# A four-layer attention and feed-forward network on one core: inputs by batch, and a new order around the first router

## What is computed

```python
# layer 0, attention (per batch)
x = einsum('bdn,bdm->bnm', Q, K) / sqrt(dk)      # Q: normalised x, K: ctx
score = sigmoid(x)
out = einsum('bvn,bnm->bvm', V, score)           # V: ctx; out is added to x

# layer 0, mixture of experts (16 experts, 4 chosen for each token)
logits = x @ router_weight.T + router_bias       # x: second normalisation
top_val, top_idx = top_k(logits, 4); top_val = softmax(top_val)
gate_up = einsum('th,ehd->etd', x, gate_up_proj) + gate_up_proj_bias
out = sum over e of score[t,e] * (down_proj_e((up + 1) * gate * sigmoid(1.702 * gate)) + bias)

# layer 3, attention: the keys on the context, which the kernel computes early
kvx = einsum('bsi,oi->bso', cond, w_kv_x); kx, vx = split(kvx); kx = _ln(kx.reshape(b, sc, g, d), ...)
```

## Time and profile before

| | |
|---|---|
| median of 3 runs | 1167.55 us (1164.51 to 1169.42) |
| the profiled execution's own time | 1166.6 us |
| its span | 1164.8 us |
| mean granted clock of TensorE | 0.944 |
| busy: PE, PEld, DVE, ACT, POOL | 88%, 75%, 74%, 54%, 47% of the span |
| chain that ended last, by engine | PE 64%, DVE 19%, ACT 10%, issue 4%, POOL 1%, DMA 1% |
| instructions | 18816 |

### The profile page before, as it was taken

How to read it: one execution, slowest core, us unless ns; L and a number is a source line. 1 busy time by engine, 2 the same in 40 slices (tenths; PEclk the granted TensorE clock), 3 DMA queues, 4 the chain that set the end, 5 groups by cost and what they waited for, 6 DMA issues and landing times.

```text
span 1164.8 us, 18816 instructions
## 1 busy us (share of the span) xinstructions
PE 1026.3 (88%) x6446; PEld 872.4 (75%) x6446; DVE 862.2 (74%) x2151; ACT 628.7 (54%) x1656; POOL 549.5 (47%) x413
## 2 busy tenths in 40 slices
PE   4999999999995897877488599999999999999976
PEld 4648888888884684545255488899889988999955
DVE  4436777777778544569887688888888888888873
ACT  1474444444432353577845477676666667675621
POOL 2316766577642221101233565655746575645550
PEclk9899999999997898878798799999999999999998
DMA  6003011111000101000000000001010101000101
GB/s 253 1 1 104 28 55 46 37 55 55 28 1 25 37 17 37 36 2 1 12 8 19 24 31 19 20 1 55 1 38 2 55 2 37 2 19 1 74 0 37
DMA packets 13680, 37.14 MB, mean 32 GB/s; under 512 B 1345, under 2 KB 5521, under 8 KB 12945
## 3 DMA queue, kind: packets, MB, share of 16 engines
q1 hardware_dynamic: 13584, 35.93, 9.3%
HBM read 34.88 MB, written 1.05 MB: 31 GB/s over the span
## 4 chain that ended last, share of the span: by engine, by line
PE 64%; DVE 19%; ACT 10%; issue 4%; POOL 1%; DMA 1%; SPq 0%; DVEq 0%; ACTq 0%; POOLq 0%
PE bank L680 15%; PE bank L700 7%; PE bank L2041 6%; PE bank L2064 6%; PE bank L1979 6%; ACT y L2187 3%; PE bank L1954 3%; PE bank L1990 3%; PE bank L1041 2%; DVE g_ql L1913 2%; PE bank L1056 1%; PE bank L1968 1%; PE bank L490 1%; DVE g_bs L2345 1%; PE bank L491 1%
## 5 line engine op out<-in xcount | busy, mean ns | idle before, releaser
L2187 ACT ACTIVATE y<-bank,g_mx 128x256 f32<-128x256 f32 x256 | 117.5, 486 | 98.6 <-DVE g_mx L2357 98.6
L2476 POOL TENSOR_TENSOR y<-y,g_sm 128x1024 f32<-128x1024 f32 x64 | 120.0, 1895 | 21.9 <-DVE g_sm L2365 21.9
L2453 POOL TENSOR_TENSOR g_c<-arena 128x1024 fp32r<-128x1024 f32 x30 | 64.1, 2136 | 115.7 <-DVE arena L2289 115.7
L2064 PE MATMUL bank<-arena 128*128 128x256 f32 x512 | 116.1, 379 | 0.0
L718 ACT ACTIVATE arena<-arena 128x512 f32<-128x512 f32 x64 | 40.4, 633 | 126.2 <-DVE arena L799 126.2
L2064 PEld LDWEIGHTS bank<-arena 128*128 128x128 f32 x512 | 94.9, 190 | 12.0 <-issue 0.2
L680 PE MATMUL bank<-b_yh,b_wh 128*128 128x512 f32 x256 | 102.6, 401 | 0.0
L680 PE MATMUL bank<-b_yl,b_wh 128*128 128x512 f32 x256 | 101.9, 398 | 0.0
L680 PE MATMUL bank<-b_yh,b_wl 128*128 128x512 f32 x256 | 101.6, 397 | 0.0
L2041 PE MATMUL bank<-g_qh,g_xs 128*128 128x256 f32 x256 | 68.0, 301 | 22.3 <-POOL g_xs L2420 15.8
L753 POOL TENSOR_TENSOR b_hl<-arena,b_hh 128x512 fp32r<-128x512 f32 x64 | 81.4, 1293 | 9.0 <-ACT b_hh L727 9.0
(11 more groups left out here) (380 smaller groups left out, 3139.9 us busy)
## 6 DMA issues: line engine op xcount, KB each, us to landing
arena<-in_dram SPq DMA_DIRECT2D x37, 512.0 KB, 3.6
arena<-in_dram SPq DMA_DIRECT2D x17, 256.0 KB, 3.8
arena<-in_dram SPq DMA_DIRECT2D x3, 1024.0 KB, 4.9
cx<-in_dram SPq DMA_DIRECT2D x2, 1024.0 KB, 8.2
arena<-in_dram SPq DMA_DIRECT2D x2, 704.0 KB, 7.3
x<-in_dram SPq DMA_DIRECT2D x1, 1024.0 KB, 5.6
cxT<-in_dram SPq DMA_DIRECT2D x1, 1024.0 KB, 11.2
out_dram<-x SPq DMA_DIRECT2D x4, 256.0 KB, 2.2
```

Of the source, the lines that this page charges most:

```text
L2064: m = pe.matmul(o[:, st * 256:st * 256 + 256], g_t[:, c, st * P:st * P + P], keys, start=True, stop=True)
L2187: m = act.activation(g_p[:, c, st, :], o[:, st * 256:st * 256 + 256], ACT.Exp, bias=g_mx[j % 2][:, 2 * c + st:2 * c + st + 1], accum_out=g ...
L2453: pool.tensor_tensor(cat, g_o[j % 2], g_om, ALU.subtract).then_inc(s_gc, 1)
L2476: pool.tensor_tensor(pf, pf, sums, ALU.mult).then_inc(s_gp, 1)
```

## The change

On SyncE the three inputs come in by batch (x, `cx`, `cxT` of batch 0, then of batch 1, and so on), the constants behind them, `rows` last; each has a semaphore of its own. On the DVE, `A_dve` now holds both normalisations and the additions by batch: each batch of the first normalisation is opened and scaled before the next, and the second normalisation of a batch is opened right after its addition. `setup_dve` and `G_consts_dve` stand in `B_dve` behind the routing steps, `K_centre_dve` behind the opening of batch 0 of the second normalisation. On POOL the centring of the key weights comes in two parts between batches of the second normalisation, and the all-reduce behind the first expert's low part. On TensorE the router's 16 matmuls of 16 columns become two rows of two matmuls with 512 columns and 16 output partitions, copied by ACT to `b_sT` and transposed back by eight transposes; the first six key products stand between them.

```diff
@@ setup_dve @@
-            dve.wait_ge(s_cst, 48)
+            dve.wait_ge(s_cst, 16)
...
-            dve.wait_ge(s_ctxT, 16)
+            for b in range(B):
+                dve.wait_ge(s_ctxT[b], 16)
@@ A_pe @@
-            pe.wait_ge(s_ctx, 16)
-            pe.wait_ge(s_ctxT, 16)
-            pe.wait_ge(s_cst, 48)
...
                     o = claim(pe, ("A", "s", b))
+                    pe.wait_ge(s_ctx[b], 16)
                     pe.wait_ge(s_y, 8 * K_A + 2 * b + 2)
...
                     have(pe, ("A", "s", c))
+                    pe.wait_ge(s_ctxT[c], 16)
@@ A_dve @@
+        def A_add_dve(dve, b):
+            o = take(dve, ("A", "o", b))
+            xb = x[:, 2 * b:2 * b + 2, :].rearrange("p t d -> p (t d)")
+            empty(dve.tensor_tensor(xb, xb, o[:, :], ALU.add), ("A", "o", b))
+            have(dve, ("A", "o", b))
+
         def A_dve(dve, V):
             for b in range(B):
-                o = take(dve, ("A", "o", b))
-                xb = x[:, 2 * b:2 * b + 2, :].rearrange("p t d -> p (t d)")
-                empty(dve.tensor_tensor(xb, xb, o[:, :], ALU.add), ("A", "o", b))
-            for b in range(B):
-                have(dve, ("A", "o", b))
+                dve.wait_ge(s_x[b], 16)
+                ln_open_batch(dve, V, b)
+                if b == B - 1:
+                    A_add_dve(dve, 0)
+                ln_scale(dve, K_A, b)
+            ln_open_batch(dve, V, 0)
+            K_centre_dve(dve, V)
+            ln_scale(dve, K_B, 0)
+            A_add_dve(dve, 1)
+            ln_open_batch(dve, V, 1)
+            A_add_dve(dve, 2)
+            ln_open_batch(dve, V, 2)
+            ln_scale(dve, K_B, 1)
+            A_add_dve(dve, 3)
+            ln_open_batch(dve, V, 3)
+            ln_scale(dve, K_B, 2)
+            ln_scale(dve, K_B, 3)
@@ K_centre_pool @@
-        def K_centre_pool(pool):
+        def K_centre_pool(pool, part):
             pool.wait_ge(s_kcs, 1)
-            for k in range(KD):
+            for k in (part,):
@@ B_pe @@
-            yt_pe(pe, K_B, "B")
+            def logits(h):
+                o = claim(pe, ("B", "lgT", h))
+                have(pe, ("B", "yt", 2 * h))
+                have(pe, ("B", "yt", 2 * h + 1))
+                for k in range(KD):
+                    m = pe.matmul(o[0:NE, :], b_rw[:, k, :], yT[:, k, h * 512:h * 512 + 512], start=(k == 0),
+                                  stop=(k == 1))
+                fill(m, ("B", "lgT", h))
+
+            pe.wait_ge(s_cst, 16)
             pe.wait_ge(s_small, 32)
+            yt_pe(pe, K_B, "B", range(3))
+            logits(0)
+            K_raw_pe(pe, 0)
+            K_raw_pe(pe, 1)
+            yt_pe(pe, K_B, "B", (3,))
+            K_raw_pe(pe, 2)
+            logits(1)
+            K_raw_pe(pe, 3)
             o = claim(pe, ("B", "lg"))
-            for b in range(B):
-                have(pe, ("B", "yt", b))
+            have(pe, ("B", "lgT", 0))
+            have(pe, ("B", "lgT", 1))
             for t in range(T):
-                for k in range(KD):
-                    m = pe.matmul(o[:, t * NE:t * NE + NE], yT[:, k, t * P:t * P + P], b_rw[:, k, :],
-                                  start=(k == 0), stop=(k == 1))
+                m = pe.transpose(o[:, t * NE:t * NE + NE], b_sT[0:NE, t * P:t * P + P], ident[0:NE, 0:NE])
             fill(m, ("B", "lg"))
+            for n in range(4, K_EARLY):
+                K_raw_pe(pe, n)
@@ B_act @@
-            yt_act(act, "B")
+            def logits(h):
+                o = take(act, ("B", "lgT", h))
+                empty(act.copy(b_sT[0:NE, h * 512:h * 512 + 512], o[0:NE, :]), ("B", "lgT", h))
+
+            yt_act(act, "B", range(3))
             split_y_act(act, 0)
+            logits(0)
+            K_raw_act(act, 0)
+            K_raw_act(act, 1)
+            yt_act(act, "B", (3,))
+            K_raw_act(act, 2)
             split_e_act(act, 0)
+            logits(1)
+            K_raw_act(act, 3)
             split_y_act(act, 1)
-            for n in range(K_EARLY, 11):
+            for n in range(4, 11):
                 K_raw_act(act, n)
@@ B_pool @@
             split_e_pool(pool, 0)
+            ctx_quant_pool(pool, C)
             K_rstd_pool(pool, C, 0)
@@ B_dve @@
             dve.tensor_tensor(lgf, lgf, b_m8[:, :, 0:1].to_broadcast([P, T, NE]), ALU.subtract).then_inc(s_blg, 1)
             V.sync()
+            setup_dve(dve, V)
+            G_consts_dve(dve, V)
             dve.wait_ge(s_bex, 1)
@@ block.sync @@
-            sp.dma_start(x[:, :, :], x_d.rearrange("b (h p) d -> p (b h) d", p=P)).then_inc(s_x, 16)
+            for b in range(B):
+                t2, ts_ = slice(2 * b, 2 * b + 2), slice(256 * b, 256 * b + 256)
+                sp.dma_start(x[:, t2, :], x_d[b].rearrange("(h p) d -> p h d", p=P)).then_inc(s_x[b], 16)
+                sp.dma_start(cx[:, t2, :], ctx_d[b].rearrange("(h p) d -> p h d", p=P)).then_inc(s_ctx[b], 16)
+                sp.dma_start(cxT[:, :, ts_], ctxT_d[:, :, ts_]).then_inc(s_ctxT[b], 16)
             sp.dma_start(cst[:, :], cst_d).then_inc(s_cst, 16)
-            sp.dma_start(cols[:, :], cols_d).then_inc(s_cst, 16)
-            sp.dma_start(rows[:, :], rows_d.partition_broadcast(P)).then_inc(s_cst, 16)
-            sp.dma_start(cx[:, :, :], ctx_d.rearrange("b (h p) d -> p (b h) d", p=P)).then_inc(s_ctx, 16)
-            sp.dma_start(cxT[:, :, :], ctxT_d).then_inc(s_ctxT, 16)
+            sp.dma_start(cols[:, :], cols_d).then_inc(s_cols, 16)
             sp.dma_start(k_w, wkx_d).then_inc(s_kw, 16)
             sp.dma_start(b_rw[:, :, :], rw_d).then_inc(s_small, 16)
             sp.dma_start(b_bd[0:NE, :], bd_d).then_inc(s_small, 16)
+            sp.dma_start(rows[:, :], rows_d.partition_broadcast(P)).then_inc(s_rows, 16)
@@ programs of the engines @@
-            for n in range(K_EARLY):
-                K_raw_pe(pe, n)
...
-            dve.wait_ge(s_x, 16)
-            ln_dve(dve, V, K_A)
-            setup_dve(dve, V)
-            K_centre_dve(dve, V)
-            G_consts_dve(dve, V)
             A_dve(dve, V)
             done()
-            ln_dve(dve, V, K_B)
             B_dve(dve, V)
...
             ln_pool(pool, C, K_A, EPS)
-            ctx_quant_pool(pool, C)
-            K_centre_pool(pool)
-            ln_pool(pool, C, K_B, EPS)
+            ln_pool(pool, C, K_B, EPS, batches=(0,))
+            K_centre_pool(pool, 0)
+            ln_pool(pool, C, K_B, EPS, batches=(1,))
+            K_centre_pool(pool, 1)
+            ln_pool(pool, C, K_B, EPS, batches=(2, 3))
```

More of the change, by code:

```diff
@@ L200, in build @@
         s_dve, s_act, s_pool = sem("dve_done"), sem("act_done"), sem("pool_done")
-        s_x, s_ctx, s_ctxT, s_cst = sem("x_loaded"), sem("ctx_loaded"), sem("ctxT_loaded"), sem("cst_loaded")
+        s_x, s_ctx, s_ctxT = ([sem(f"{n}_loaded{b}") for b in range(B)] for n in ("x", "ctx", "ctxT"))
+        s_cst, s_cols, s_rows = sem("cst_loaded"), sem("cols_loaded"), sem("rows_loaded")
         s_stage, s_out = sem("stage_done"), sem("stored")
@@ L468, in K_centre_dve @@
         def K_centre_dve(dve, V):
+            dve.wait_ge(s_cols, 16)
             k0 = COLS["kw"][0]
@@ L597, in build @@
             plan(("B", "yt", b), b % 4)
+        for h in range(2):
+            plan(("B", "lgT", h), 6 + h)
         plan(("B", "lg"), 6)
@@ L758, in B_dve @@
             o = take(dve, ("B", "lg"))
+            dve.wait_ge(s_rows, 16)
             lgf = b_lg[:, :, :]
@@ L2825, in _ @@
             A_act(act)
-            for n in range(K_EARLY):
-                K_raw_act(act, n)
             B_act(act)
```

## The result

| | before | after |
|---|---|---|
| median, us (runs) | 1166.92 (4, 1164.51 to 1169.42) | 1157.90 (4, 1157.58 to 1159.03) |
| the profiled execution's own time | 1166.6 | 1157.58 |
| its span | 1164.8 | 1155.8 |
| mean granted clock of TensorE | 0.944 | 0.948 |

The changed kernel takes 0.9936 of the time before (95% interval 0.992 to 0.9952), a saving of 0.64% or 7.5 us (the two medians alone would give 0.9923). The forecast of 1163.5 us, a saving of 3.1 us, had the sign right and under half of the size. The side on which it fell, faster by over 0.5%, had been given 0.32.

A forecast was written before the change was run, and what follows sets the result against it. TensorE bounds the kernel almost unbroken from 14.93 us, a transfer before. Ten products at 31.7 + 20.2 + 4.5 + 0.7 = 57.1, 3.1 us earlier: 1166.6 to 1163.5 us; own range 1161.5 to 1165.5, 8-in-10 range 1158.5 to 1167.5.

The forecast's parts named there:

- Part 1, the first y: Loads by batch: first y at 9.98 us, first attention matmul from 14.93 to 10.0, 4.9 us gained.
- rival 1: GpSimd ready early: its first configuration costs nothing, another 2.7 us saved at the start, 1160.8 us; chance 0.25.
- if the first costs the same: GpSimd's first configuration costing 6.7 us like two others: ready at 7.8 at the earliest; 8.10 taken.
- The spacing of the batches: First normalisation on the DVE: batches one after another at 3.05 us each.
- Part 2, the uncovered normalisation: Second normalisation, no longer hidden: TensorE idles some 4 us, first router row at 31.7, the 4.9 us lead gone.
- Rival 4: Second normalisation's DVE and GpSimd chain 2 to 4 us longer, router row slips as much; about 1166.5 us; chance 0.1.
- Part 3, low clock: From first router row to ten products: TensorE's clock falls after idling, adding 4.5 us to 20.2 of work.
- rival 3: Low clock before the ten products costs 2.8 or 0 us; 1161.8 to 1159.0 us; chance 0.15.
- The waits for ACT: TensorE waiting for ACT's copies between first router row and ten products: 0.7 us added.
- What costs nothing: Moved setup, constants, all-reduce and configurations hide in DVE and GpSimd idle time of 16.66 and 16.37 us.
- The same distances afterwards: After the ten products, distances stay as before; a change over 2 us would show the prediction wrong.
- Rival 2: Clock stays down until within the expert half: ten products 9.6 us later, 1176.2 us; chance 0.05.

The follow-up runs named there:

- x_early: The changed kernel with each later batch of x issued one place earlier; 1159.53 us, ratio 0.9951 to the kernel before.
- late_centre: The changed kernel with both key-weight centring halves behind all four roots on GpSimd; 1154.89 us, ratio 0.9915 to the kernel before.
- keep_warm: The changed kernel with four extra 512-column matmuls, two in each of TensorE's two gaps; 1157.07 us, ratio 0.9927 to the kernel before.
- reorder: The changed kernel with batch 0's second scaling behind batch 1's addition and opening, second centring half behind the roots; 1154.93 us, ratio 0.9911 to the kernel before.
- reorder_again: The kernel reorder repeated unedited in another group; 1154.95 us, ratio 0.991 to the kernel before.
- again: The changed kernel once more, unedited; 1158.31 us, ratio 0.9943 to the kernel before.
- loads_only: The kernel before with only the transfers, their semaphores and the first normalisation by batch; 1169.03 us, ratio 1.0034 to the kernel before.

## Why the prediction was right in kind and short in size

- **Part 1, the first y: wrong, by the choice of GpSimd's readiness.** I took 8.10 because two other configurations cost 6.7 each. The first one costs nothing visible, so rival 1 held: first y at 6.46, attention at 6.62. It was named with its mechanism and 2.7 us; it gave 3.4. The Trainium skill (GPSIMD Engine Reference, section 2.1, Instruction dispatch) has about 6 us for the first call of a freshly loaded kernel; here the first arithmetic came 0.2 us after its data and 3.6 us after the configuration, so no such cost shows. The failed step is "if the first costs the same". The point for rival 1, that 8.10 is only 0.17 behind the DVE's 7.93, was the better evidence.
- **The spacing of the batches: about right.** Forecast 3.05 us each (the parts named sum to 2.94); 2.82 measured, and once 1.06 more, as x of batch 1 landed only at 7.51, 5.09 after its issue. x_early shows that this cost nothing in the end.
- **Part 2, the uncovered normalisation: right, with a mechanism missing.** The wait and its releaser are as forecast. The last scaling that counts ended at 29.26, forecast 31.2; with a start 3.4 earlier it should have been 27.8. The missing 1.4 us are the collision (1.6 + 1.15 us in two scalings), less what I had allowed too much for the weight means (3.0 for 2.5), for three additions with their openings (1.8 each for 1.66) and in small amounts elsewhere. **Rival 4's mechanism was therefore true**, and by late_centre it cost 2.4 us at the last scaling and 2.9 at the ten products, in its forecast of 2 to 4; its time was not reached because rival 1 was true as well. I had made them exclusive cases, and they were independent.
- **Part 3, low clock: right that it falls, mis-sized.** 4.5 forecast; 2.1 measured from the first router row on (23.39 us to the ten products in the change, 21.31 in keep_warm), 2.65 with what stands ahead of the row. I charged the router row and the 2.8 us of a return; the return's loss includes the row, as rival 3 had it, and only one of the two returns that I took 2.8 from is one that the granted clock shows. The whole stretch was forecast as 25.4 us (31.7 to 57.1) and measured 23.4: 2.4 less of low clock, and 0.4 more of all else (21.3 in keep_warm, forecast 20.9). The waits for ACT stand at 0.7 in that forecast, though their three parts sum to 0.6.
- **What costs nothing: right.** The setup lies at 48.76 to 53.1 on the DVE, which then still waits 13.15 us for the exponential; the all-reduce runs at 51.45 and the key roots end at 65.4, 13.2 us before GpSimd is wanted. ACT's pace is unchanged: four products apart 7.38 us, as in the earlier trace rows.
- **The same distances afterwards: not quite.** 1.6 us less to the third expert half and about 1 more to the end. Together 2.6 us, over the 2 that I had named as a sign of error. By reorder and reorder_again the 1.6 can be chance in the clock, though both profiles of the change have the short value. The last 1 us is within what unedited work scatters by: from the third expert half to the end it is 1061.6 us before and 1060.6 after, but 1060.3 in again and late_centre and 1063.8 in x_early, and no edit touches it in any of them.
- **Rival 2 (the clock does not return): false** in all profiles.

The sum with measured terms: 1.3 us (first router row earlier than forecast) and 2.0 us (shorter way to the ten products) on top of 3.1 makes the 6.4 measured. The medians of again differ by 6.25 us. The 9.0 of the first pair of profiled executions has their chance in it; the range's low end of 1158.5 left little room for that, and for rivals 1 and 3 coming together. That the sum came out only 3.3 us short at the ten products is partly luck: against 3.4 us more from the start stood the collision, which was not in it.

## What to carry to other kernels

Where an engine's first row starts 0.2 us behind its input, take that input as the cause before a cost seen elsewhere in the program. When work is moved so that the DVE and GpSimd run at once, list which DVE instructions fall beside GpSimd's long ones, and let additions from PSUM and statistics stand there rather than scalings: moving the centring gained about 3 us here. And an early start pays only if the waits behind it are moved too: alone it cost 0.34% in this kernel.

## What the runs showed of the hardware

- A two-instruction scaling (fp32, 128x256 each) takes 0.73 us, and 1.88, 2.31 or 3.88 when one or both of its instructions are issued during a GpSimd instruction on 128x1024; additions with one input from PSUM (0.68) and statistics (0.75) stay as they are. This is the one thing that I had not expected in size: 1.6 us for one call on the critical chain.
- The first MODIFY_POOL_CONFIG of the program costs nothing visible; behind those to and from the all-reduce stand 6 to 7.3 us without work where nothing else hid them (5.97 and 7.31 in loads_only, 6.67 and 6.72 before, 7.13 after).
- The same unedited instructions take 41.4, 43.0 or 44.5 us from the ten products to the third expert half, in steps of about 1.5 us with the granted clock; 41.35 and 43.01 come from two executions of one kernel.
- The first attention matmuls take 0.63 us each where later ones take 0.38, at a granted clock that reads 1.00 (before, after).
